# Experts' outputs scattered by entry and added to their rows inside layer 1, whose first four batches come last

## The reference, cut to what matters

```python
x = x + tanh(g_xattn[0]) * cross_attention_0(layernorm(x), ctx)      # 16 heads, with biases
x = x + tanh(g_ffn[0])   * experts(layernorm(x), expert_weights, expert_indices, w1, w2, bias)
x = x + tanh(g_xattn[1]) * cross_attention_1(layernorm(x), ctx)      # 16 heads of 64
x = x + tanh(g_ffn[1])   * prototypes(layernorm(x), ...)             # 2 nearest of 32, rank 16

def experts(x, ...):                       # 8 experts, 256 -> 1024 -> 256, two entries a token
    order = argsort(expert_indices.reshape(-1))
    tok = order // 2
    ys = ragged_dot(gelu(ragged_dot(x[tok], w1, counts)), w2, counts)
    ys = ys * flat_w[order][:, None]
    return zeros_like(x).at[tok].add(ys) + bias
```

## Time and profile before

| | |
|---|---|
| runs | 3157.91, 3158.71, 3170.38 us, median 3158.71 |
| profiled execution | 3159.7 us |
| its span in the profile | 3157.9 us |
| mean granted clock of PE | 0.973 of full speed |
| PE busy | 2797.5 us (89%) |
| PE weight loads | 2223.4 us (70%) |
| DVE busy | 2638.4 us (84%) |
| ACT busy | 1876.1 us (59%) |
| POOL busy | 2174.8 us (69%) |

### The profile page before, as it was taken

One profiled execution on the slowest core, in us unless ns is written; L12 is line 12 of the kernel. 1 busy time (PEld: TensorE's weight loads), 2 busy tenths in 40 slices (PEclk: granted clock), 3 DMA queues, 4 the chain that ended last, 5 costly groups with the idle time before them and its releaser, 6 DMA issues.

```text
span 3157.9 us, 101355 instructions
## 1 busy us (share of the span) xinstructions
PE 2797.5 (89%) x33450; PEld 2223.4 (70%) x33450; DVE 2638.4 (84%) x6696; ACT 1876.1 (59%) x3733; POOL 2174.8 (69%) x3915
## 2 busy tenths in 40 slices
PE   4889986888888888689499999999999999999997
PEld 2444444666666666557388888888888888888885
DVE  6887886888888888775489998998888999899986
ACT  2666765777777777675255555555545555555553
POOL 3892001666666666632388888888888888888887
PEclk7999997999999999899699999999999999999999
DMA  5996755322222222631434444434444434444441
GB/s 155 362 344 262 283 230 195 88 73 77 83 80 72 79 83 77 227 107 40 108 85 97 96 109 94 99 92 104 102 92 96 98 92 106 101 99 92 106 94 42
DMA packets 369334, 388.77 MB, mean 123 GB/s; under 512 B 118480, under 2 KB 344224, under 8 KB 364032
## 3 DMA queue, kind: packets, MB, share of 16 engines
q1 hardware_dynamic: 349008, 336.34, 38.4%
q0 software_dynamic: 6992, 22.45, 2.4%
q10 hardware_dynamic: 12960, 25.23, 2.2%
HBM read 235.07 MB, written 148.81 MB: 122 GB/s over the span
## 4 chain that ended last, share of the span: by engine, by line
PE 39%; DVE 6%; issue 3%; POOL 2%; ACT 2%; DVEq 0%; DMA 0%; POOLq 0%; ACTq 0%
PE banks L150 11%; PE banks L152 10%; PE banks L151 10%; PE banks L1193 3%; PE banks L1178 2%; DVE a_probT_lo L1288 1%; PE banks L1225 1%; ACT a_qT_hi L1069 1%; DVE a_pick L1426 1%; DVE a_y L1445 1%; PE banks L1248 1%; DVE a_rsum L1313 1%; DVE a_wsel L1435 0%; PE banks L1240 0%; ACT a_ynT_hi L1069 0%
## 5 line engine op out<-in xcount | busy, mean ns | idle before, releaser
L1069 ACT ACTIVATE a_qT_hi<-banks 128x512 f16<-128x512 f32 x256 | 152.8, 597 | 707.0 <-PE banks L152 707.0
L383 POOL TENSOR_TENSOR a_probT_lo<-a_expT,a_probT_hi 128x512 f16<-128x512 f32 (+1 forms) x384 | 371.9, 998 | 244.1 <-ACT a_probT_hi L458 244.1
L449 ACT ACTIVATE a_expT<-banks,a_top,w_score_scale 128x512 f32<-128x512 f32 (+1 forms) x384 | 272.2, 709 | 111.8 <-PE banks L544 111.8
L967 POOL TENSOR_TENSOR a_pn<-a_prob,a_rsum 128x1024 f32<-128x1024 f32 (+1 forms) x256 | 307.1, 1221 | 4.9 <-DVE a_rsum L1315 4.0
L150 PE MATMUL banks<-a_xnT_hi,w_q_hi 128*128 128x256 f16 x1024 | 282.2, 276 | 4.5 <-DVE a_xnT_lo L1286 4.5
L150 PE MATMUL banks<-a_vo_front,a_probT_hi 128*128 128x256 f16 x1024 | 279.3, 273 | 2.8 <-DVE a_probT_lo L1288 2.6
L152 PE MATMUL banks<-a_xnT_hi,w_q_lo 128*128 128x256 f16 x1024 | 281.7, 275 | 0.0
L151 PE MATMUL banks<-a_xnT_lo,w_q_hi 128*128 128x256 f16 x1024 | 281.5, 275 | 0.0
L152 PE MATMUL banks<-a_vo_front,a_probT_lo 128*128 128x256 f16 x1024 | 279.3, 273 | 0.0
L151 PE MATMUL banks<-a_vo_front,a_probT_hi 128*128 128x256 f16 x1024 | 279.3, 273 | 0.0
L1288 DVE SCALAR_TENSOR_TENSOR a_probT_lo<-banks,a_probT_hi 128x512 f16<-128x512 f32 (+1 forms) x384 | 212.8, 582 | 42.2 <-ACT a_probT_hi L1069 42.1
(11 more groups left out here) (392 smaller groups left out, 10623.5 us busy)
## 6 DMA issues: line engine op xcount, KB each, us to landing
vo<-kv_vo_out SPq DMA_DIRECT2D x38, 2048.0 KB, 7.5
a_vo_front<-vo SPq DMA_DIRECT2D x128, 512.0 KB
kt<-kv_k_out ACTq DMA_DIRECT2D x9, 2560.0 KB, 15.0
a_k<-kt SPq DMA_DIRECT2D x64, 308.0 KB, 3.6
kv_raw_e<-in_L_ffn_w POOLq DMA_DIRECT2D x16, 1024.0 KB, 9.7
a_x<-in_x SPq DMA_DIRECT2D x64, 256.0 KB, 3.0
a_y<-in_x SPq DMA_DIRECT2D x64, 256.0 KB, 2.8
x<-a_y SPq DMA_DIRECT2D x64, 256.0 KB, 2.2
```

The costliest lines, as they stand in the source:

```text
L383: pool.tensor_tensor(probT[b][1][0:rows, first:end, :], expT[b][0:rows, first:end, :], probT[b][0][0:rows, first:end, :], ALU.subtract).th ...
L449: act.activation(expT[1 - h][0:rows, first:end, :], bank, ACT.Exp, bias=top[0:rows, 0:1], scale=weights["score_scale"][0:rows, 0:1]).then_ ...
L967: last = pool.tensor_tensor(keys_of(pn[h]), keys_of(prob_of(u, h, 2)), rsum[h][:, :].unsqueeze(2).broadcast_to([P, H, n]), ALU.mult)
L1069: act.activation(out, bank[:, 0:cols].rearrange("p (c s) -> p c s", c=out.shape[1]), ACT.Copy, scale=scale)\
```

## The change

It has two halves.

In the expert stage, the outputs go to memory in the order of the entries, not of the slots. `token_of` gets a second column: beside the token, the row of `outputs_of` to which the slot's output belongs, which is 2 x token + k for the k-th entry of a token, and a row behind all entries for a slot without one. `outputs_of` grows by those rows. GpSimd scatters each tile of 128 outputs by that column (L2517), six tiles behind the gathers (Y_LATE), for which moe_y has eight tiles in place of three; 17 scatters stand in the loop and six behind it. SyncE issues only weight loads. The gathers of L2500, the adds of L2705, the load of the 1024 rows, the weights and bias, and the eight stores of L2466 are gone from this stage, which ends once the scatters have landed.

In layer 1, batches are taken in another order: body i works on batch i + 4, and the last four bodies on batches 0 to 3 (`batch_at`, `tile_at`). In the first 16 bodies SyncE handles the experts' eight tiles of 128 rows beside its own work: at the end of an even body it loads 128 rows of `x1` (a_first_x) and the 256 rows of `outputs_of` that belong to them (a_first_y), at the end of an odd body it stores the sum. VectorE forms that sum at the end of the even bodies, in `add_experts`: rows plus gated bias, plus each of the two outputs times its gated weight. Before it loads batch 0's rows in the last four bodies, SyncE waits until all sums are stored (`first_stored`).

```diff
 def attention_ffn_phase(...)
+    batch_at = lambda i: i + FIRST - NB if isinstance(i, int) and i + FIRST >= NB else i + FIRST
...
         def load_x(i, u, j):
             n, _ = turn(u, j, X_SLOTS)
             need(sp, xn_ready, i - X_SLOTS + 1)
-            sp.dma_start(x_sb[n][:, :, :], src[i]).then_inc(x_in[n], 16)
+            if isinstance(i, int) and i == NB - FIRST:
+                for p in range(2):
+                    sp.wait_ge(first_stored[p], 16 * MOE_TILES // 2)
+            sp.dma_start(x_sb[n][:, :, :], src[batch_at(i)]).then_inc(x_in[n], 16)
+
+        def load_first(n):
+            p = n % 2
+            need(sp, first_stored[p], 16 * (n // 2))
+            sp.dma_start(first_x[p][:, :], src_rows[n]).then_inc(first_in[p], 16)
+            sp.dma_start(first_y[p][:, :, :], expert_rows[n * TOPK * P:(n + 1) * TOPK * P].rearrange("(p k) d -> p k d", k=TOPK))\
+                .then_inc(first_in[p], 16)
+
+        def store_first(n):
+            sp.wait_ge(first_ready, n + 1)
+            sp.dma_start(src_rows[n], first_x[n % 2][:, :]).then_inc(first_stored[n % 2], 16)
...
         def body(i, u, j):
...
                     need(sp, out_ready, t + 1)
-                    sp.dma_start(dst[t], y_sb[slot][:, :]).then_inc(out_done[slot], 16)
+                    sp.dma_start(dst[tile_at(t)], y_sb[slot][:, :]).then_inc(out_done[slot], 16)
...
                 if h == 0 and live(i, NB):
                     load_values(i, u, j)
+            if isinstance(i, int) and i < TPB * MOE_TILES:
+                if i % 2 == 0:
+                    load_first(i // 2)
+                else:
+                    store_first(i // 2)
...
+            if isinstance(i, int) and i < TPB * MOE_TILES and i % 2 == 0:
+                add_experts(i // 2)
+
+        def add_experts(n):
+            p = n % 2
...
+            dve.wait_ge(first_in[p], 32 * (n // 2 + 1))
+            step = Steps(dve, first_step, n, TOPK)
+            step(nc.vector.tensor_tensor(first_x[p][:, :], first_x[p][:, :], first_bias[:, :], ALU.add))
+            for k in range(TOPK):
+                last = nc.vector.scalar_tensor_tensor(out=first_x[p][:, :], in0=first_y[p][:, k, :], scalar=first_w[:, n, k:k + 1],
+                                                      in1=first_x[p][:, :], op0=ALU.mult, op1=ALU.add)
...
 def expert_phase(...), SyncE
-        for j in range(J):
-            if j == 3:
-                sp.wait_ge(w_ready, 10)
-                load_weights(second_load)
-            if j == E:
-                sp.wait_ge(w_ready, 2 * E)
-                layer1.sync_loads()
-            sp.wait_ge(y_ready, j + 1)
-            sp.dma_start(outputs_of[j * P:(j + 1) * P], y_sb[j % 3][:, :]).then_inc(y_stored[j % 3], 16)
-        for t in range(MOE_TILES):
-            sp.wait_ge(added, TOPK * (t + 1))
-            sp.dma_start(rows[:, t, :], xm[:, t, :]).then_inc(out_done, 16)
-        sp.wait_ge(out_done, 16 * MOE_TILES)
+        sp.wait_ge(w_ready, 10)
+        load_weights(second_load)
+        sp.wait_ge(w_ready, 2 * E)
+        layer1.sync_loads()
...
 def expert_phase(...), GpSimd
+        def scatter(j):
+            pool.wait_ge(y_ready, j + 1)
+            pool.indirect_dma_start(outputs_of, bass.IndirectOffsetOnAxis(ap=token[:, j, 1:2], axis=0), y_sb[j % Y][:, :],
+                                    None).then_inc(y_stored[j % Y], 16)
...
                 gather(j + GATHERS)
+            if j >= Y_LATE:
+                scatter(j - Y_LATE)
...
         layer1.gpsimd_tops()
-        for n in range(3):
-            pool.wait_ge(y_stored[n], 16 * ((J - n + 2) // 3))
-        for s in range(ENTRIES):
-            n = s % YG
-            need(pool, added, s - YG + 1)
-            pool.indirect_dma_start(yg[n][:, :], None, outputs_of, bass.IndirectOffsetOnAxis(ap=slot[:, s:s + 1], axis=0))\
-                .then_inc(yg_in[n], 16)
+        for j in range(J - Y_LATE, J):
+            scatter(j)
+        for n in range(Y):
+            pool.wait_ge(y_stored[n], 16 * ((J - n + Y - 1) // Y))
...
 def expert_phase(...), VectorE, behind the last tile
         layer1.vector_turned()
-        dve.wait_ge(gated, 3)
-        for s in range(ENTRIES):
-            t, n = s // TOPK, s % YG
-            dve.wait_ge(yg_in[n], 16 * (s // YG + 1))
-            need(dve, added, s)
-            nc.vector.scalar_tensor_tensor(out=xm[:, t, :], in0=yg[n][:, :], scalar=wts[:, s:s + 1], in1=xm[:, t, :],
-                                           op0=ALU.mult, op1=ALU.add).then_inc(added, 1)
```

More of the change, by code:

```diff
@@ L783, in attention_ffn_phase @@
     hwT = pair("hwT", [P, LC, P])
+    first_x = [sb(f"first_x{n}", [P, D]) for n in range(2)]
+    first_y = [sb(f"first_y{n}", [P, TOPK, D]) for n in range(2)]
+    first_w, first_bias = sb("first_w", [P, MOE_TILES, TOPK]), sb("first_bias", [P, D])
     ps_scores = psum[:, 0:3 * BANK]
@@ L788, in attention_ffn_phase @@
     x_in = [sem(f"x_in{n}") for n in range(X_SLOTS)]
+    first_in = [sem(f"first_in{n}") for n in range(2)]
+    first_stored = [sem(f"first_stored{n}") for n in range(2)]
+    first_w_in, first_gated, first_step, first_ready = (
+        sem("first_w_in"), sem("first_gated"), sem("first_step"), sem("first_ready"))
     k_in = [sem(f"k_in{p}") for p in range(2)]
@@ L1923, in _ @@
         pool.wait_ge(scattered, 16 * ENTRIES)
-        with nc.allow_non_contiguous_dma("tokens of the slots, one value per partition"):
-            pool.dma_start(route["token"][:, :], token_of.rearrange("(j p) a -> p (j a)", p=P)).then_inc(tokens_in, 16)
+        with nc.allow_non_contiguous_dma("tokens and entries of the slots, two values at a time"):
+            pool.dma_start(route["token"][:, :, :], token_of.rearrange("(j p) a -> p j a", p=P)).then_inc(tokens_in, 16)
         pool.wait_ge(tops0_set, 3)
@@ L2414, in expert_phase @@
     hT = sb("hT_hi", [P, FC, P], F16), sb("hT_lo", [P, FC, P], F16)
-    y_sb = [sb(f"y{n}", [P, D]) for n in range(3)]
-    yg = [sb(f"yg{n}", [P, D]) for n in range(YG)]
+    y_sb = [sb(f"y{n}", [P, D]) for n in range(Y)]
     xbank = [psum[:, n * BANK:n * BANK + D] for n in range(2)]
@@ L2420, in expert_phase @@
     ybank = [psum[:, (6 + n) * BANK:6 * BANK + n * BANK + D] for n in range(2)]
-    power_set, x_in, small_in, w_in = sem("power_set"), sem("x_in"), sem("small_in"), sem("w_in")
+    power_set, w_in = sem("power_set"), [sem(f"w_in{e}") for e in range(AHEAD, E)]
     xg_in = [sem(f"xg_in{n}") for n in range(GATHERS)]
@@ L2753, in flamingo_layers @@
             wq, score_scale, ffn = layer1.results()
[L2754 to L2755 removed]
+            attention_ffn_phase(nc, layer, psum, const, batches(x1), tiles(x1), tiles(out), keys(DC, KV_COLS // P),
+                                (out_front, out_back), wq, score_scale, ffn,
+                                (outputs_of, ins["L0_ffn_expert_weights"], ins["L0_ffn_bias"]))
 _INS = ["x", "ctx_1024", "g_xattn", "g_ffn", "L0_xattn_w_q", "L0_xattn_b_q", "L0_xattn_w_k", "L0_xattn_b_k",
```

90 lines of the change are left out of this document (44 added, 46 removed).

## The result

| | before | changed |
|---|---|---|
| median of the runs | 3161.33 us (4 runs, 3157.91 to 3170.38) | 3187.09 us (4 runs, 3185.73 to 3193.35) |
| profiled execution, its span | 3159.7, 3157.9 us | 3187.15, 3185.4 us |
| mean granted clock | 0.973 | 0.974 |

The ratio is 1.0081, 95% interval 1.0055 to 1.0107: slower, by about 26 us. The prediction was 3187 us. Whether it was right for its reasons is read from the traces.

A forecast was written before the change was run, and what follows sets the result against it. In layer 1 PE is nearly always busy and waits on VectorE behind a_y; the tail leaves PE idle. Six holds of 8.15 us, 49.6 with body 2, less 22.5 give +27.1 on 3159.7: 3187 us, range 3168 to 3202.

The forecast's parts named there:

- The seam and what bounds it: Between expert stage and layer 1: the tail of gathers, adds and stores goes, gain 22.5 us (20 to 23.7).
- both end together: End of expert stage: last scatter lands at 1507.1, VectorE's weight work ends at 1507.58; new stage 1.2 us later.
- GpSimd in the expert stage, cost nothing: Expert stage: the scatters fit into GpSimd's 71.4 us of waits for moe_xn; cost nothing, at worst 2 us.
- A microsecond of VectorE behind a_y is one of PE: Layer 1, body's end: PE's next product waits for a_probT_lo behind a_y, so added VectorE time there delays PE equally.
- The load is issued behind the wait for out_ready: Ends of bodies 4 to 14: SyncE loads only after a_y sets out_ready, so VectorE waits 4.5 us (4.0 to 6.8).
- Bodies 0 and 2 cost 0.7: Layer 1's start: no wait for loads; body 0 costs 0 (up to 2), body 2's adds 0.7 us (0 to 1.5).
- The clock, 2.2 us a hold: Layer 1, behind each hold: 4.4 us of work at the slow clock, 2.2 us lost (0 to 3.4).
- the accident at 2315: Earlier trace, a loop's turn: a_rsum 3.04 us late cost 6.5 us, read as hold plus 3.4 of slow clock.
- Absorption: Layer 1: VectorE's spare 2.3 us per 25 cover the adds and loads come early; 3137 to 3149, chance 8%.
- The clock staying up (3174): Layer 1: holds cost only their length, 5.95 us each, clock stays at 2.4 GHz; +13.9 us, chance 13%.
- Holds longer than forecast: Layer 1: wait of 5.5 us and 3.4 lost to the clock per hold; +40, 3200 us, chance 12%.
- The tail went in part: End of expert stage: last scatter lands late, gain 15 in place of 22.5; +34.6, 3194 us, chance 5%.

The follow-up runs named there:

- first experiment: Changed kernel, but SyncE issues the a_first_x and a_first_y loads at the even body's start; sums stay behind a_y: 3146.6 us against 3160.2, ratio 0.9956.
- the sweep: Changed kernel with loads a body ahead and sums behind a_y, plus 1 to 11 more VectorE instructions in bodies 4 to 14: 3179.9 us, one execution.

## Why the prediction was right, step by step

- **The seam and what bounds it.** Right that the tail was all path; its size was 2.3 us too large, 22.5 against 20.2. The step that failed is "both end together" with 1.2 us for the change of stage. The 1.2 was right behind VectorE (1.23 measured) and the landing of 3.7 was too long (2.65), but GpSimd's end of the stage, 4.8 us, was not in the sum. The earlier trace rows do not show it, since before the change SyncE's stores were last. It was nearly last there too: GpSimd's last gather was issued by 1525.82, and 4.7 us more make 1530.5, 0.8 ahead of the new stage.

```profile
1531.31 0.20 POOL L947 MEMSET a_wsel<- 128x128 f32 x1 [5.50 <-POOLq L2746]
```

  The tail was within the bounds given (20 to 23.7).
- **GpSimd in the expert stage, cost nothing.** Right. From the last attention tile to the last moe_y it took 176.7 us with the scatters (1330.6 to 1507.3) and 178.8 without, but that is no gain, for the kernel before with the table alone, which has no scatters either, took 176.8. GpSimd's waits for moe_xn fell from 71.4 to 52.9, so the spare time paid. The scatters' row:

```profile
L2517 POOL DMA_INDIRECT outputs_of<-moe_y,route_token x23: 962/1006/2893, 1384.4 to 1508.1; - x23
```

  The longest, 2.4, 2.0 and 2.9 us, are the first three, and each ends 0.9 us behind a weight split of VectorE that began 0.3 to 1.2 us before it:

```profile
1400.11 2.35 DVE L2692 SCALAR_TENSOR_TENSOR wall<-wall,route_inverse 128x2048 f16<-128x2048 f32 x1 [1.26 <-ACT wall L2620]
1400.44 2.89 POOL L2517 DMA_INDIRECT outputs_of<-moe_y,route_token  x1 [0.30 <-issue]
```

  The split ends at 1402.46, the issue at 1403.33. The next scatter, at 1408.84 with no split beside it, took 0.99. And a gather that began just before a split took no longer than usual:

```profile
1391.28 1.02 POOL L2512 DMA_INDIRECT route_rows<-x,route_token  x1 [3.61 <-DVE moe_xn L2679]
1391.40 2.35 DVE L2692 SCALAR_TENSOR_TENSOR wall<-wall,route_inverse 128x2048 f16<-128x2048 f32 x1 [0.41 <-ACT wall L2620]
```

  These times agree with what the Trainium skill describes ("SBUF — State Buffer", "Who interferes with whom"): of VectorE in a 2-port mode and GpSimd, the one that issues first holds the shared port to its end. Whether the split runs in such a mode, as the prediction took for granted, no run shows. Its price was 0, not 2, since GpSimd had the time.
- **A microsecond of VectorE behind a_y is one of PE.** Right, and shown twice: 1.55 us of sum cost 1.52 (first experiment), a hold of 2.93 cost 2.91 (the sweep).
- **The load is issued behind the wait for out_ready.** Right: 4.57 us of wait each, forecast 4.5. The second load's issue began 1.4 us behind a_y's end in four of the six, as forecast, and 1.9 and 2.2 us behind it in the others. By the medians the two loads landed in 2.2 and 2.8 us. The estimate of 2.6 worked out from the Trainium skill ("DMA: Bandwidth & Descriptors", "Anatomy of one DMA — SWDGE (gpsimd) path") was as near to the second as the 3.0 taken from a_x; but the skill gives that fit for transfers that GpSimd issues, and these are SyncE's.
- **Bodies 0 and 2 cost 0.7.** Measured 0.2 with all else up to body 3. Kernels without any sum took 99.7 to 101.5 us for this stretch, so 0.2 can't be told from 0 or from 0.7. Only bodies 4 to 14 have holds, as the order of SyncE's list said.
- **The clock, 2.2 us a hold.** Measured 1.7: the six costs (46.6 us above 11.38 each) less the six holds (a_y to a_rsum, 36.2). The forecast rested on the accident at 2315, which was called one "of the same kind". It was not. There PE stops twice, at 2314 and at 2318, at the turn of a loop, and the profile names nothing but PE's own issue as what ended either stop:

```profile
2316.53 1.09 PE L1193 MATMUL banks<-ident,a_pn 128*128 128x128 f32 x8 [2.23 <-issue]
...
2319.62 0.31 PE L1178 MATMUL banks<-a_k,a_qT_hi 64*128 64x77 f16 x3 [1.74 <-issue]
```

  A plain hold of 2.93 cost 2.91, not 6.5. That the 2.2 came out near the truth is in part luck: it was a choice, below the accident's 3.4 and towards the two other stretches of the earlier trace rows. Its way of counting, half of the slow time that falls on work, fits the first hold. There the rows of the clock make 4.5 and 5.8 us at 1.2 GHz, about 5 of them behind PE's return at 1648.61, and 2.3 us were lost beyond the hold.
- **The sum.** Tail -20.2 (forecast -22.5), holds and body 2 +47.7 (forecast +49.6), and +4.4 and -4.4 in stretches that the change doesn't touch in any way I could show. That two misses of 2 us cancel is luck, and so is that +4.4 and -4.4 do; that the misses are small is not. Nor does the agreement of the totals, 3187 and 3187.1, say more than the terms do: the sum started from one execution of the kernel before, 3159.7, and the medians differ by 25.8 us, not by the forecast 27.1.
- **Rivals.** Absorption is ruled out by the first experiment, where even 1.5 us show in full. The clock staying up (3174) is ruled out by the 0.64 above; with holds of 1.5 us it does stay up. Holds longer than forecast were not met (6.0 us each with the sums, forecast 5.95). The tail went in part, but by 2.3 us and by another way than a late scatter. "By that rule shorter holds than forecast would keep it up", which the prediction says of the Trainium skill's "The HAM clock gate" ("TensorE: Matmul & The Clock Gate"), was half right: at 1.5 us all six did, at 2 to 3 us one of two, and that was the longer one.
- **The range.** Its lower end takes 5.5 us a hold where the terms' low bounds, 4.0 and 1.3, make 5.3. That changes +9.3 to +8.1, and 3168 is what the latter gives.

## What to carry to other kernels

An average busy share says nothing about a point. Ask the chain of waits where an engine's next instruction frees what the bottleneck wants, and put extra work anywhere but there: six times the same three instructions cost 9.3 us behind a_y and 1.5 in gaps earlier in the same half. For each load that an engine will wait for, look in the issuing queue for a wait on that same engine ahead of it; moving the issue one body up was worth 38 of the 47 us. And where a stage ends with GpSimd waiting for its transfers, let another engine do the waiting; here that began the next stage 1.7 us sooner.

## What the runs showed of the hardware that I had not expected

- GpSimd takes 4.7 to 4.8 us from its last instruction or wait of the expert stage to the start of the next; behind VectorE it is 1.2.
- Of two holds of PE on VectorE, 2.0 and 2.9 us, the shorter brought TensorE's clock down from 2.4 to 1.2 GHz for 3 to 4 us (0.83 on average over 10 us), the longer did not (1.00). In all holds in which it fell, here and in the changed kernel, it cost 1.1 to 2.5 us beyond the hold.
- The same first stage ends at about 510 or about 516 us, with the same code.
- An indirect DMA that GpSimd begins to issue while VectorE runs a weight split takes 2.0 to 2.9 us and ends 0.9 us behind the split; begun 0.1 us before the split, it takes 1.0.
